# A decoder of twelve layers: the expert blocks of one mixture layer taken in pairs for the second product

## The reference

```python
E, K, I = (64, 8, 192)
logits = x @ gate_weight.T
scores = softmax(logits)
topk_w, topk_idx = top_k(scores, K)
topk_w = topk_w / sum(topk_w)
# tokens sorted by expert, 512 features each
g = ragged_dot(sorted_tokens, w_gate, group_sizes)     # 512 -> 192
u = ragged_dot(sorted_tokens, w_up, group_sizes)       # 512 -> 192
out = ragged_dot(silu(g) * u, w_down, group_sizes)     # 192 -> 512
y = sum(outs * topk_w, axis=1)
```

## Time and profile before

| | us |
|---|---|
| median of three runs | 6170.57 |
| lowest and highest | 6168.83, 6171.36 |
| the profiled execution | 6156.4 |
| its span, first to last instruction | 6155.2 |
| PE busy | 4739.6 (77%) |
| DVE busy | 3361.0 (55%) |
| POOL busy | 1789.3 (29%) |
| ACT busy | 1542.1 (25%) |

### The profile page before, as it was taken

How to read it: one execution, slowest core, us unless ns; L and a number is a source line. 1 busy time by engine, 2 the same in 40 slices (tenths; PEclk the granted TensorE clock), 3 DMA queues, 4 the chain that set the end, 5 groups by cost and what they waited for, 6 DMA issues and landing times. The chain is left out here.

```text
span 6155.2 us, 65534 instructions
## 1 busy us (share of the span) xinstructions
PE 4739.6 (77%) x23622; PEld 2649.7 (43%) x23653; DVE 3361.0 (55%) x5406; ACT 1542.1 (25%) x2993; POOL 1789.3 (29%) x1747
## 2 busy tenths in 40 slices
PE   7997888899965742387789888734999997886487
PEld 4664444344433632154433333322555554343276
DVE  4555767667749986899534444451222223345622
ACT  1111666411111100243222222200111111343132
POOL 0002222001126667144201111145555554001411
PEclk9997999999985555688899999857999998897598
DMA  1000000100000002200000000023788776001000
GB/s 73 1 1 8 2 2 2 66 0 0 0 9 0 0 0 28 98 7 1 19 1 15 4 1 8 1 91 98 199 212 207 185 176 155 5 1 66 2 1 28
DMA packets 109695, 272.25 MB, mean 44 GB/s; under 512 B 19057, under 2 KB 22769, under 8 KB 106930
## 3 DMA queue, kind: packets, MB, share of 16 engines
q0 software_dynamic: 46880, 100.30, 8.5%
q1 hardware_dynamic: 62498, 167.76, 7.9%
HBM read 345.47 MB, written 67.96 MB: 67 GB/s over the span
## 5 line engine op out<-in xcount | busy, mean ns | idle before, releaser
L204 PE MATMUL ps<-arena 128*128 128x512 f32 (+19 forms) x19083 | 4174.0, 449 | 793.7 <-DMA arena<-in_L_gamma 82.1
L204 PEld LDWEIGHTS ps<-arena 128*128 128x128 f32 (+6 forms) x19114 | 2071.7, 166 | 2575.9 <-issue 1391.0
L209 PE MATMUL ps<-arena 128*128 128x128 f32 (+3 forms) x3515 | 502.2, 279 | 569.8 <-DMA arena<-moe_x,arena 155.8
L209 PEld LDWEIGHTS ps<-arena 128*128 128x128 f32 (+3 forms) x3515 | 403.0, 143 | 827.9 <-issue 562.6
L253 POOL TENSOR_SCALAR arena<-arena 128x1 f32<-128x1 f32 x192 | 74.0, 386 | 1591.3 <-DVE arena L247 1591.1
L2536 POOL DMA_INDIRECT moe_y<-arena x191 | 302.2, 1582 | 414.0 <-DVE arena L2495 379.9
L1969 DVE TENSOR_REDUCE arena<-ps 128x2 f32<-128x256 f32 (+3 forms) x256 | 199.0, 820 | 351.2 <-PE ps L204 351.2
L789 DVE TENSOR_REDUCE arena<-ps 128x2 f32<-128x1024 f32 x256 | 304.5, 1219 | 153.1 <-PE ps L204 152.8
L2484 DVE SCALAR_TENSOR_TENSOR arena<-ps,arena 128x192 f32<-128x192 f32 x191 | 79.7, 417 | 545.1 <-ACT arena L2370 545.1
L1948 ACT ACTIVATE arena<-ps 128x1024 f32<-128x1024 f32 (+3 forms) x256 | 166.2, 701 | 558.2 <-PE ps L204 558.2
L765 ACT ACTIVATE arena<-ps 128x512 f32<-128x512 f32 x512 | 277.9, 596 | 87.0 <-PE ps L204 82.2
(11 more groups left out here) (297 smaller groups left out, 4211.6 us busy)
## 6 DMA issues: line engine op xcount, KB each, us to landing
arena<-in_L_ffn_gu SPq DMA_DIRECT2D x191, 768.0 KB
arena<-in_L_ffn_dn SPq DMA_DIRECT2D x191, 384.0 KB
moe_y<-arena SPq DMA_DIRECT2D x8, 1024.0 KB
arena<-moe_y SPq DMA_DIRECT2D x8, 1024.0 KB
arena<-in_L_ffn_w SPq DMA_DIRECT2D x8, 1024.0 KB
arena<-in_x SPq DMA_DIRECT2D x4, 1024.0 KB
arena<-in_L_attn_W_qkvu SPq DMA_DIRECT2D x4, 1024.0 KB
arena<-in_L_ffn_up_w SPq DMA_DIRECT2D x4, 1024.0 KB
```

Source lines behind the costliest of these rows:

```text
L204: return self.nc.tensor.matmul(out, lhsT, rhs, start=start, stop=stop, skip_group_check=True)
L209: return self.nc.tensor.transpose(out, in_, ident[0:n, 0:n])
```

## The change

Blocks 2q and 2q + 1 form pair q (block 190 is alone). The 192 hidden units are cut in 128 and 64, not in 96 and 96. A product over the 128 units uses all rows of the array. The other 64 units of the even block lie on the lower half of the partitions, those of the odd block on the upper half, so that one transpose turns both, and the two products over 64 units address the two halves of the array. They add to the banks that the products over 128 units began. Steps 4, 5 and 6 run once per pair, in the round of its odd block; the function `blocks` makes that list. The weights of the second product come in two transfers: 256 KB as before (only for the first block of an expert), and 128 KB for every block, into the half that the block's parity tells. The scaling on DVE is two instructions, for 128 and for 64 columns. The buffer of h and its transpose hold a pair. The results of `down` have four buffers instead of three.

```diff
-    GU, DN = k.alloc([NW, 4, 384]), k.alloc([NW, 2, 512])
+    GU, DN, DB = k.alloc([NW, 4, 384]), k.alloc([NW, 512]), k.alloc([NW, 512])
-    SG, HH = ([k.alloc([192]) for _ in range(2)] for _ in range(2))
-    HT = [k.alloc([2, P]) for _ in range(2)]
-    YG = [k.alloc([512]) for _ in range(3)]
+    SG, HH = [k.alloc([192]) for _ in range(2)], [k.alloc([3, P]) for _ in range(2)]
+    HT = [k.alloc([3, P]) for _ in range(2)]
+    YG = [k.alloc([512]) for _ in range(4)]
...
             sp.wait_ge(pe, "down", n - NW)
-            dma.start(sp, DN[0:96, bass.ds(slot, 1)].rearrange("p s a b -> p (s a b)"),
-                      wd[bass.ds(e, 1)].rearrange("a p n -> p (a n)"), "dn", n, cond=first > 0)
+            dma.start(sp, DN[:, bass.ds(slot, 1)].rearrange("p s b -> p (s b)"), wd[bass.ds(e, 1), 0:P].rearrange("a p n -> p (a n)"),
+                      "dn", n, cond=first > 0)
+            sp.wait_ge(pe, "down", n - 2 * NW)
+            dma.start(sp, DB[64 * (n % 2):64 * (n % 2) + 64, n // 2 % NW, :], wd[bass.ds(e, 1), P:192].rearrange("a p n -> p (a n)"),
+                      "db", n)
...
+    def blocks():
+
+        for s, n in skew(NB, BLOCK):
+            if s < 4:
+                yield s, n
+            elif n % 2 or n == NB - 1:
+                yield s, n // 2
+
+    def pair(q):
+
+        return [(n, slice(64 * (n % 2), 64 * (n % 2) + 64)) for n in range(2 * q, min(2 * q + 2, NB))]
...
             elif s == 4:
-                r = R.take("ht", n, by=((dve, "ht", n),))
-                pe.wait_ge(dve, "h", n)
-                for c in range(2):
-                    t = k.tr(r[0:96, c * P:c * P + P], HH[n % 2][:, 96 * c:96 * c + 96])
-                t.then_inc(*pe.done("ht", n))
+                q = n
+                r = R.take("ht", q, by=((dve, "ht", q),))
+                pe.wait_ge(dve, "h", pair(q)[-1][0])
+                for n, half in pair(q):
+                    k.tr(r[:, n % 2 * P:n % 2 * P + P], HH[q % 2][:, n % 2, :])
+                wide = half.stop
+                k.tr(r[0:wide, 2 * P:3 * P], HH[q % 2][:, 2, 0:wide]).then_inc(*pe.done("ht", q))
             elif s == 5:
-                r = R.take("down", n, by=((dve, "y", n),))
-                pe.wait_ge(dve, "ht", n)
-                pe.wait_ge(dma, "dn", n)
-                for c in range(2):
-                    t = k.mm(r, HT[n % 2][0:96, c, :], DN[0:96, bass.ds(slots[n], 1), c, :], c == 0, c == 1)
-                t.then_inc(*pe.done("down", n))
+                q = n
+                y = [R.take("down", n, by=((dve, "y", n),)) for n, _ in pair(q)]
+                pe.wait_ge(dve, "ht", q)
+                for n, _ in pair(q):
+                    pe.wait_ge(dma, "dn", n)
+                    k.mm(y[n % 2], HT[q % 2][:, n % 2, :], DN[:, bass.ds(slots[n], 1), :], True, False)
+                for n, _ in pair(q):
+                    pe.wait_ge(dma, "db", n)
+                for n, half in pair(q):
+                    k.mm(y[n % 2], HT[q % 2][half, 2, :], DB[half, q % NW, :], False, True).then_inc(*pe.done("down", n))
...
-        for s, n in skew(NB, BLOCK):
+        for s, n in blocks():
             if s == 3:
                 dve.wait_ge(act, "silu", n)
                 dve.wait_ge(dma, "tb")
-                dve.wait_ge(pe, "ht", n - 2)
-                nc.vector.scalar_tensor_tensor(out=HH[n % 2], in0=R.of("up", n)[:, 192:384], scalar=TB[:, n, 1:2], in1=SG[n % 2],
-                                               op0=ALU.mult, op1=ALU.mult).then_inc(*dve.done("h", n))
+                dve.wait_ge(pe, "ht", n // 2 - 2)
+                h, up, c = HH[n // 2 % 2], R.of("up", n)[:, 192:384], n % 2 * 64
+                for to, of in ((h[:, n % 2, :], slice(0, P)), (h[:, 2, c:c + 64], slice(P, 192))):
+                    nc.vector.scalar_tensor_tensor(out=to, in0=up[:, of], scalar=TB[:, n, 1:2], in1=SG[n % 2][:, of], op0=ALU.mult,
+                                                   op1=ALU.mult).then_inc(*dve.done("h", n))
             elif s == 4:
-                dve.wait_ge(pe, "ht", n)
-                dve.wait_ge(pe, "down", n - 2)
-                nc.vector.tensor_copy(HT[n % 2][0:96], R.of("ht", n)[0:96, 0:256].rearrange("p (c n) -> p c n", c=2)).then_inc(
-                    *dve.done("ht", n))
+                q = n
+                dve.wait_ge(pe, "ht", q)
+                dve.wait_ge(pe, "down", 2 * q - 3)
+                if len(pair(q)) == 2:
+                    nc.vector.tensor_copy(HT[q % 2], R.of("ht", q)[:, 0:3 * P].rearrange("p (c n) -> p c n", c=3)).then_inc(
+                        *dve.done("ht", q))
+                else:
+                    nc.vector.tensor_copy(HT[q % 2][:, 0, :], R.of("ht", q)[:, 0:P]).then_inc(*dve.done())
+                    nc.vector.tensor_copy(HT[q % 2][0:64, 2, :], R.of("ht", q)[0:64, 2 * P:3 * P]).then_inc(*dve.done("ht", q))
             elif s == 5:
-                dve.wait_ge(pe, "down", n)
-                if n >= 3:
-                    dve.queue.wait_ge(sums_in[(n - 3) % 2], 16 * ((n - 3) // 2 + 1))
-                nc.vector.tensor_copy(YG[n % 3], R.of("down", n)).then_inc(*dve.done("y", n))
+                for n, _ in pair(n):
+                    dve.wait_ge(pe, "down", n)
+                    if n >= 4:
+                        dve.queue.wait_ge(sums_in[n % 2], 16 * ((n - 4) // 2 + 1))
+                    nc.vector.tensor_copy(YG[n % 4], R.of("down", n)).then_inc(*dve.done("y", n))
...
             elif s == 6:
-                pool.wait_ge(dve, "y", n)
-                if n >= 2:
-                    pool.queue.wait_ge(sums_in[n % 2], 16 * (n // 2))
-                nc.gpsimd.indirect_dma_start(YD[n % 2], bass.IndirectOffsetOnAxis(ap=TB[:, n, 0:1].bitcast(U32), axis=0), YG[n % 3], None,
-                                             compute_op=ALU.add).then_inc(sums_in[n % 2], 16)
+                for n, _ in pair(n):
+                    pool.wait_ge(dve, "y", n)
+                    if n >= 2:
+                        pool.queue.wait_ge(sums_in[n % 2], 16 * (n // 2))
+                    nc.gpsimd.indirect_dma_start(YD[n % 2], bass.IndirectOffsetOnAxis(ap=TB[:, n, 0:1].bitcast(U32), axis=0), YG[n % 4],
+                                                 None, compute_op=ALU.add).then_inc(sums_in[n % 2], 16)
...
-    d["L2_ffn_dn"] = np.asarray(a["L2_ffn_w_down"]).reshape(NE, 2, 96, 512).transpose(0, 2, 1, 3).reshape(NE, 96, 1024)
+    d["L2_ffn_dn"] = np.asarray(a["L2_ffn_w_down"])
```

## The result

The changed kernel takes 6233.69 us, median of three runs (6225.89 to 6242.40), where the kernel before takes 6170.57: a ratio of 1.0103, 95% interval 1.0080 to 1.0126. It is slower, as forecast, but by 63 us and not by 31. The profiled execution of after is the median one; its span is 6232.4 us, 77.2 more than that of before.

The account below looks back on a forecast made before the run. TensorE, busy 920 of 920 us, bounds the stage. Per pair +0.89 wait, -0.45 half products, -0.11 transposes = +0.33, times 95.5 = +31 us: 6187 against the profile, 6202 at the median; range 6160 to 6240, own range 6185 to 6215.

Parts of the forecast that it names:

- Half products: Second product on PE: 64-row halves run side by side, half part 1.27 us, saving 0.45 us a pair.
- the 0.09: PE, second product: extra 0.09 us when going from 128-row matmuls into the 64-row ones.
- The 32-row groups: Attention-stage matmuls, four groups side by side, used as stand-in for 64-row pairs: 1.08 us at 512 columns.
- the rival with the halves one after another: Second product on PE: halves don't overlap, +113 us, or +71 if the inner two do; 6242 to 6283; chance 0.10.
- The sum: PE, per pair: 0.89 stall less 0.45 and 0.11 saved gives +0.33 us, times 95.5 = +31 us.
- the 0.21: Half part on PE: 0.21 us of its 1.08 in which the array changes shape and loads weights openly.
- Transposes: Transposes of the hidden units on PE: four a pair become three, 0.45 to 0.33 us, saving 0.11.
- The wait for h: PE ahead of `ht` at odd steps, waiting for silu and scaling: 0.89 us a pair, bounds 0.69 and 0.96.
- this 0.13: DVE scaling ahead of `ht`: as two instructions it ends 0.13 us later, all added to PE's stall.
- the one costed at nothing, SP: SyncE's weight loads: `gu` queued behind the even block's `dn` has 10 us, needs 3.4, so isn't late; 0 us.
- waits for the weight loads: PE waiting for weights in the steady part: listed as a sign that the forecast is wrong, without a size.
- rival 5: PE's clock falls to 0.97 granted because of idle gaps: +29 us more, 6231; chance 0.06.

Follow-up runs that it names:

- the run on one half: Changed kernel with SP's loads and PE's steps reordered, both 64-unit products of a pair reading the lower half of the array: 6204.06 us.
- the faster version: Changed kernel with the next pair's `gu` loads ahead of this pair's `dn` and `db`, `up` before `down` in even rounds, `gx` one round earlier: 6124.27 us.
- the difference of two runs: Changed kernel with `gu` loads moved ahead, 6194.22 us, against the same with `up` also before `down` and `gx` a round earlier, 6124.27 us.
- the version with the weights ahead: Changed kernel with only SP's order altered, the next pair's `gu` loads ahead of this pair's `dn` and `db`: 6194.22 us.
- the same new order of PE: `up` before the pair's `down` in even rounds, `gx` a round earlier: 6124.27 us with `gu` loads moved ahead, 6574.83 us with the changed kernel's SP queue.

## Why the prediction was right in sign and short in size

**Half products.** Right. From the last 128-row load before to the first half load 0.95 = 0.43 + 0.52, as the 0.09 said; 1.06 from there to the next 128-row load, which the prediction put at 1.08; 0.10 of open load after it (4405.337 to 4405.764 between the first two matmuls of `up`, 0.43 against 0.32). The 32-row groups were a good stand-in, and the rival with the halves one after another is excluded by the run on one half, at +80 us. One reading of the rows was too narrow: the prediction has 0.09 "each way", but they show it on the way in only. On the way out 0.64 less two passes of 0.22 leaves about 0.2, as here (1.06 - 0.86), in which the change of shape and the open load aren't told apart. The sum had the 0.21 right.

**Transposes.** Right: in the faster version seven take 0.82 (4400.23 to 4401.05), 0.12 each, and a pair has one `ht` transpose fewer.

**The wait for h.** Right in kind and place, 95 times and ended by DVE, but 0.76 us a pair by the difference of two runs, where the sum took 0.89. From `gx` to `ht` it is 4409.18 - 4408.02 = 1.16 us, 0.72 more than the 0.44 without a wait; the fill of before had 0.69. The two scalings did end 0.13 later than one would have (4408.59 + 0.54, so 1.11 after `gx` began, against 0.98 in the fill), yet `ht` started 0.05 after that end, where it had started 0.15 after it in the fill: of the 0.13 added for the second instruction 0.03 arrived. The term mis-sized is this 0.13. The net of a pair is +0.22 and not +0.33: 21 us, not 31. Why `ht` starts closer behind the scaling here no run shows.

**The step that failed** is the one costed at nothing, SP: "it has two steps, 10 us, instead of three", and its loads "take 3.4 us alone, so it is not late". Two things were left out of it. The two steps start at the wait for the pair's `down`, and SP's own time stands behind that wait: the issues of `dn` and `db` and three register loads, so that `gu` is issued 3.9 us after the start of the second half products. And the load was priced by the queue's rate alone, 3.4 us, where a `gu` load took 5.0 us in the median already before and 7.4 in the odd blocks after. 3.9 + 7.4 = 11.3 against 10.7 is late in the median, and there were 25 waits for the 35 odd loads: 35 us, with 3 for the second block and 4 for the clock 42. Both parts were needed: 3.9 + 5.0, or 2.2 + 7.4, would have been in time in the median. That the loads got longer could not be read from the kernel before; the 5.0 and its 8.3 at most could, and 3.9 + 8.3 is over 10.7. That this would be seen as "waits for the weight loads" was written down; no rival gave it a price.

**The fill** was not in the sum: 10 us in the profile, 8 by the medians for what brings it.

**The clock.** Granted 0.99 in the steady part and 0.97 from 4800 to 4900 us. It fell to its lower level three times, each within 1 us of the end of a wait for `gu` of 2.2 to 2.7 us, and not at the waits for h: the version with the weights ahead keeps 1.00 with all of those. So that the time came near the 6231 of rival 5 is coincidence: the clock cost 4 us and not 29. The forecast's own range, 6185 to 6215, was missed.

**The sum, as it should have been:** 21 + 42 + 10 is 73, beside 77 between the profiles. Against the medians, +63, it is too much, since the profiled execution of before was 14 us faster than its median and that of after was not. Two more single executions of before gave 6158.72 and 6155.70, again below all those of the repeated runs (6161.48 and more). What these do differently no profile shows.

## What to carry to other kernels

Where a change makes a step rarer, everything queued behind a wait for that step comes later by the whole interval, on the DMA-issuing engine too; count that engine's register loads and issues in the chain as one counts matmuls, and take a load's time from loads under the stage's traffic, not from bandwidth. Even then leave room: the same load took 5.0 us in one queue and 7.4 to 7.7 in another with the same or little more traffic. A pair step frees and fills the pipeline in lumps: put independent products between its producer and its consumer, and check each queue before the order of another is changed, since here the same new order of PE was 70 us faster with one queue of SP and 335 us slower with the other.

## What the runs showed of the hardware

- Going from 128-row to 64-row products costs 0.09 us, also when only one half of the array is used; two halves side by side cost 0.85 us less for four 512-column passes than the same on one.
- Three register loads with their checks take 1.7 us of SyncE's queue, a transfer of 64 partitions and 128 KB 0.52 to issue.
- A load of 768 KB took 5.0 us in the median before and 7.7 where the load behind it was split in two, with the same bytes in all; why is open.
- A stretch of 13 to 17 SyncE instructions at 0.7 or 1.4 us each came in each profile with a third transfer in the loop and in none of the three without; 15 or 96 more instructions ahead of it left it where it was in the program.
- With 56 waits of 5.8 us in 1290 us the clock was granted at 0.85; with PE idle 92 times for 0.6 us in 955 us it stayed at 1.00.
